# The causal mask of the self attention as a bf16 product on TensorE instead of a minimum on VectorE

## What is computed

```python
def attn(x, qkv_w, o_w):
    b, s, d = x.shape
    hd = d // H
    qkv = (x @ qkv_w.T).reshape(b, s, 3, H, hd).transpose(2, 0, 3, 1, 4)
    q, k, v = (qkv[0], qkv[1], qkv[2])
    a = jnp.einsum('bhqd,bhkd->bhqk', q, k) * hd ** (-0.5)
    mask = jnp.triu(jnp.ones((s, s), dtype=bool), 1)
    a = jax.nn.softmax(jnp.where(mask, -1000000000.0, a), axis=-1)
    out = jnp.einsum('bhqk,bhkd->bhqd', a, v).transpose(0, 2, 1, 3).reshape(b, s, d)
    return out @ o_w.T
...
x = x + attn(rmsnorm(x, n1_w), qkv_w, o_w)
x = x + moe(rmsnorm(x, n2_w), gate_w, up_w, down_w)
```

## Time and profile before

| | |
|---|---|
| median of three runs | 2839.97 us |
| profiled execution | 2830.95 us |
| its span, first to last instruction | 2829.7 us |
| mean granted clock of TensorE | 0.975 |
| TensorE matmuls busy | 2597.7 us, 92% |
| VectorE busy | 2187.3 us, 77% |
| ScalarE busy | 1684.6 us, 60% |
| GpSimd busy | 1134.9 us, 40% |
| minimum with the mask, L727 | 64 instructions, 78.3 us, from 1326.6 to 2562.1 us |

### The profile page before, as it was taken

How to read it: one execution, slowest core, us unless ns; L and a number is a source line. 1 busy time by engine, 2 the same in 40 slices (tenths; PEclk the granted TensorE clock), 3 DMA queues, 4 the chain that set the end, 5 groups by cost and what they waited for, 6 DMA issues and landing times.

```text
span 2829.7 us, 60900 instructions
## 1 busy us (share of the span) xinstructions
PE 2597.7 (92%) x23748; PEld 2122.2 (75%) x23748; DVE 2187.3 (77%) x4794; ACT 1684.6 (60%) x4539; POOL 1134.9 (40%) x1981
## 2 busy tenths in 40 slices
PE   7797989899888989999899999999999999999999
PEld 5676767677666767777777777888787878788777
DVE  7868697877678587786767777787878787778998
ACT  4565666666555666666555555655656565656544
POOL 2132323323443543324454444333333333435676
PEclk9898999999899999999999999999999999999999
DMA  6000000000011121100012121100000000000110
GB/s 189 3 24 9 18 13 18 14 13 18 11 48 40 63 77 42 30 16 24 11 46 62 55 76 58 33 19 20 21 16 21 16 24 13 24 3 25 33 36 21
DMA packets 84168, 92.15 MB, mean 33 GB/s; under 512 B 15332, under 2 KB 77288, under 8 KB 83880
## 3 DMA queue, kind: packets, MB, share of 16 engines
q1 hardware_dynamic: 75432, 59.91, 6.9%
q0 software_dynamic: 8448, 28.34, 3.4%
HBM read 65.36 MB, written 22.85 MB: 31 GB/s over the span
## 4 chain that ended last, share of the span: by engine, by line
PE 63%; DVE 23%; ACT 5%; POOL 4%; issue 3%; DMA 1%; SPq 1%; DVEq 0%; POOLq 0%; ACTq 0%
PE psum L353 14%; PE psum L377 12%; PE psum L346 12%; PE psum L403 6%; DVE tiny L730 4%; PE psum L415 3%; PE psum L532 3%; DVE big L738 3%; PE psum L370 3%; PE psum L360 3%; PE psum L367 2%; PE psum L526 2%; PE psum L513 2%; DVE xn L711 1%; DVE tiny L766 1%
## 5 line engine op out<-in xcount | busy, mean ns | idle before, releaser
L377 PE MATMUL psum<-ident,big 128*128 128x128 f32 x2784 | 428.2, 285 | 66.2 <-ACT big L1219 22.4
L377 PEld LDWEIGHTS psum<-ident,big 128*128 128x128 f32 x2784 | 324.0, 145 | 140.2 <-ACT big L1219 49.3
L1219 ACT ACTIVATE big<-big 128x512 f32<-128x512 f32 x512 | 312.1, 631 | 170.4 <-DVE big L738 168.5
L730 DVE TENSOR_REDUCE tiny<-psum 128x8 f32<-128x1024 f32 x256 | 312.3, 1220 | 47.5 <-PE psum L403 42.8
L738 DVE TENSOR_TENSOR big<-psum,tiny 128x512 f32<-128x512 f32 x512 | 329.6, 685 | 8.8
L1382 POOL TENSOR_SCALAR tiny<-mv 128x1 f32<-128x1 f32 x224 | 53.0, 236 | 677.1 <-DVE mv L701 674.9
L403 PE MATMUL psum<-head_keys,small 64*128 64x256 f32 x2048 | 285.9, 403 | 19.7 <-ACT big L1226 10.9
L1399 POOL TENSOR_TENSOR head_keys<-big,head_rows 128x512 f32<-128x512 f32 x256 | 266.6, 1060 | 0.0
L1424 POOL TENSOR_TENSOR big<-big,tiny 128x512 f32<-128x512 f32 x128 | 133.8, 1052 | 308.2 <-DVE tiny L773 308.0
L403 PEld LDWEIGHTS psum<-head_keys,small 64*128 64x128 f32 x2048 | 185.3, 189 | 74.6 <-issue 56.9
L1263 ACT ACTIVATE big<-psum,tiny 128x128 f32<-128x128 f32 x512 | 181.7, 382 | 38.1 <-DVE tiny L768 37.6
(11 more groups left out here) (334 smaller groups left out, 6616.7 us busy)
## 6 DMA issues: line engine op xcount, KB each, us to landing
ctxT<-in_ctxT SPq DMA_DIRECT2D x64, 128.0 KB, 2.2
after_L_xattn<-x SPq DMA_DIRECT2D x64, 128.0 KB, 1.7
mixture_out<-spare SPq DMA_DIRECT2D x46, 128.0 KB, 1.7
x_in<-in_x SPq DMA_DIRECT2D x32, 128.0 KB, 2.2
mixture_in<-xn SPq DMA_DIRECT2D x32, 128.0 KB, 1.7
x_in<-after_L_xattn SPq DMA_DIRECT2D x32, 128.0 KB, 2.1
w_bits<-after_L_xattn SPq DMA_DIRECT2D x32, 128.0 KB, 2.1
spare<-in_L_w SPq DMA_DIRECT2D x2, 1024.0 KB, 7.2
```

Source lines behind the costliest of these rows:

```text
L377: last = pe.transpose(bank[:, k * P:(k + 1) * P], src[:, k * P:(k + 1) * P], identity)
L730: dve.tensor_reduce(top, s8, AX.X, ALU.max).then_inc(*t.dve.tell(p, f"{l}.top{r}"))
L1219: last = act.activation(flat, flat, ACT.Exp, scale=DH ** -0.5)
```

## The change

The minimum on VectorE is gone, with its signal. In its place TensorE lays the mask first: for each group of eight scores of the self attention it multiplies the bf16 identity by `m.future`, a bf16 tile of four copies of the mask (0 where a key may be seen, -4e9 where not), into each of the two banks, 128 x 512 each, with the start flag. The score products then accumulate on it. `m.future` is made once in the setup by one more VectorE instruction. The turns in `ORDER` stand in another sequence on all five engines, with the same number of turns for each lane; of these only the place is marked here.

```diff
@@ SPREAD @@
-SPREAD = {"L2": "clip", "self": "mask"}
+SPREAD = {"L2": "clip"}
@@ ORDER @@
...
@@ pe_heads @@
             pe.wait_ge(*t.act.at(p, f"{l}.eT1"))
+        if l == "self":
+            for half in range(2):
+                pe.matmul(t.ab[:, half, :], m.ident_bf[:], m.future[:].rearrange("p h s -> p (h s)"), start=True, stop=False)
         keys = t.head_keys[r].rearrange("p h s -> p (h s)")
         for cols in (slice(0, D), slice(D, 2 * D)):
             for half in range(2):
                 rows = slice(half * P // 2, (half + 1) * P // 2)
-                last = pe.matmul(t.ab[:, half, cols], t.qT[rows, r, :], keys[rows, cols], start=True, stop=True)
+                last = pe.matmul(t.ab[:, half, cols], t.qT[rows, r, :], keys[rows, cols],
+                                 start=l != "self", stop=l != "self" or cols.start > 0)
@@ dve_heads @@
-        if l == "self":
-            dve.tensor_tensor(s8, s8, m.causal[:].rearrange("p (o s) -> p o s", o=1).to_broadcast([P, 2 * CH, S]),
-                              ALU.min).then_inc(*t.dve.tell(p, f"{l}.mask{r}"))
-            dve.wait_ge(*t.dve.at(p, f"{l}.mask{r}"))
         dve.tensor_reduce(top, s8, AX.X, ALU.max).then_inc(*t.dve.tell(p, f"{l}.top{r}"))
@@ dve_constants @@
     dve.tensor_scalar(m.before[:], m.causal[:], 0.0, None, ALU.is_le)
+    dve.tensor_scalar(m.future[:], m.causal[:].rearrange("p (o s) -> p o s", o=1).to_broadcast([P, CH, S]), 0.0, None, ALU.min)
@@ shared_memory @@
+    m.future = sb("future", [P, CH, S], BF16)
```

More of the change, by code:

```diff
@@ L172 @@
[L172 to L176, removed]
@@ new lines @@
+        "1310112320023023002312310320212312021013320232120333122030132231011010130333122212001203120032010303"
+        "1221032132321212310300201313133231201201310210313023202011321123020303220230303021202332132102330120"
+        "2122303131300021020331033210010111200120323023010131230232302001023323213121313103022132021102130320"
+        "1131012312023130203011301122030230212003130212320210330123223203103010213332130102011112310302020130"
+        "2101032132323221212312313132332323002001312312312311212013201312123210301131130220332023221201203303"
@@ new lines @@
+        "1232220300301302131121330033210201221102130230210301120212300231031203020103010302101203001301313313"
+        "3221031020213130232010230211213201301212131302312103110323002202023023123212010033022322301303103103"
+        "0101330233021221220010212103023010130212020102200310031232132133011022121031213021203010232112120210"
+        "1213212013301230022011032131230232033313031322022010331311010303030230120310321001013313310021020200"
+        "2313113100220023121322130203201101302031120132231001232013121010202012111012232103110221303123212312"
@@ new lines @@
+        "0313130202221012313223201033032210020233130320123010310202201121323311312131212313232121233322323230"
+        "2000323120311300120231100201031220130312130100202231320212121231033032113023032210020113221231003012"
+        "2012030211130231203012332031321030130312310012131030303010203211213230121000123022133231001303122310"
+        "0213203301210201232120100212101210122120301220110102320231300202131231003011010323101212320210331032"
+        "0320323012232003123203231003202102013310301210133210130303031303211221020123101333002030102210313213"
@@ new lines @@
+        "1202102332032113231320211203213210120103302202301221110020231230023110310332101203232310132031013023"
+        "2032101321232002132032310002330230102133013132103103001023101033313120231321002010223012103313223213"
+        "1023201200113231321312120312211123031022301310212330203211013313001303120302101220230132230302133322"
+        "1002023312323010313021022023113030031321132031201210012032210020133132231300302012012023132313010021"
+        "2101213220121113221323202112030103332112200213310131323003021203012303122320210323020310201202332310"
@@ new lines @@
+        "0310310320110201323331123010103130121032201201303223203021320203120130312323101201013122132033213211"
+        "1323123021132130310303102322020101323100132203102113031202320212303203023122103013012002311333010320"
+        "1120230312132021010330230322123010231201323300201312010202311302203131213102023230123121132313031130"
+        "3032022213003013120010130323102102330321231130232012021030123213310132002330310120330103231231231213"
+        "0310012203278087223002708232007872878039a09730a7098a739a98a90a807893a079a789a303a9783a7098a987033739"
@@ new lines @@
+        "1121032330321323223010230330012130101100230221233233031032013012010310113233102311212203212302202010"
+        "3030301231378783207873802337382a97a98709a987a09a089a907a807398a0777a9a089878370909a09a78a39789a73bac"
+        "b98c70cbac8b98a97cab780bac9b8ca89a7bc978a87a89a09cb9c0b65956b9bc6b9c65cb659bc965bc689a856abc57b68756"
+        "c9b5c65796abc65b5a65ab6b95ab659c7965c7b68bc786cb5ca56c68a5cb69b6c9a6ba59a65b68c8b56c5875c87b58b57b76"
+        "57c6a5ac7658a7c8c567c865b5cb7c575b6c576b6ab56a5cb67ac587968cb95b685a96ca5bc9769858a65c69856"
@@ L268 @@
[L268 to L271 removed]
+        "1203332223111100023112210313223301011221131231122002322333331020300010100112233110331211211100223130"
```

170 lines of the change are left out of this document (72 added, 98 removed).

## The result

The changed kernel takes 2844.01 us (median of 20 runs, 2839.78 to 2851.94) against 2838.38 us for the kernel before on the same chip: ratio 1.0020, 95% interval 1.0013 to 1.0027, 5.6 us slower. So it is slower by 0.2 to 0.4%. The forecast was +15 us.

The account below looks back on a forecast made before the run. TensorE, 95% busy in the self attention's stretch, was taken as the bound. Added work of 31.4 us less 16 given back makes +15.4 us, 2855 us against the median 2839.97; 8 in 10 range 2832 to 2875.

Parts of the forecast that it names:

- the mask's own sum: Self attention's stretch: 31.4 us of TensorE work added, 16 us of idle time given back, net +15.4 us.
- Products 0.22 us each: TensorE, ahead of the self scores: 128 bf16 products of 512 columns at 0.22 us, 28.2 us in all.
- Weight loads at nothing: TensorE: the products' 128 weight loads hide behind the matmul ahead; without that cover at most 14 us.
- The rival of cheap wide products: TensorE: 512 columns cost no more than 256, products 14.1 us instead of 28.2, time 2841; chance 0.05.
- Added TensorE work: TensorE: products 28.2, switches of form 2.7 and setup 0.5 us, 31.4 us on an engine 95% busy.
- Switches of form: TensorE, full-array mask beside half-array scores: up to 19 of 64 groups add 0.29 us each; 2.7 us taken.
- Given back: Self attention's softmax: each lane's path shortens by 0.83 us per group, so TensorE's idle time falls by 16 us.
- The rest: Setup instruction 0.5 us; the new turns on all queues, priced in the first half, plus or minus 6 us, zero in the middle.
- Nothing is given back: TensorE's idle time stays because the order, not VectorE, makes it: 2871 us; chance 0.15.
- The lanes' latency decides: Four lanes each bound by their own path, -13 us each; TensorE 98% busy, time 2827; chance 0.12.
- It comes out even: 24.6 us of mask leave the chain, the new work lands on it only partly: about 2837; chance 0.15.
- Waits for L1219: Expected sign: the transposes' waits for ScalarE's exp in the self attention's stretch fall by some 15 us.

Follow-up runs that it names:

- e1: The changed kernel (mask as TensorE product) with the turns of the kernel before on all five queues: 2855.22 us, ratio 1.0058 to the kernel before.
- e3: The kernel before with no causal mask at all, neither minimum nor product, old turns: ratio 0.9962 to the kernel before.
- e15: e1 with 38 swaps of neighbouring turns on ScalarE only: ratio 1.0069 to the kernel before.
- e2: The kernel before, minimum still on VectorE, with the changed kernel's turns on all five queues: ratio 1.0193 to the kernel before.
- e4: The changed kernel with no causal mask at all, neither minimum nor product, new turns: ratio 0.9995 to the kernel before.
- e10: The changed kernel with 47 swaps of neighbouring turns where an engine idled while the next turn was ready: ratio 0.9997 to the kernel before.
- e13: e10 with 30 more swaps by the same rule, from its own trace: ratio 0.9988 to the kernel before.
- e5: e1 with 77 of the 128 turns of self attention's transposes one place earlier on TensorE: ratio 1.0157 to the kernel before.
- e7: The changed kernel with 125 turns of self attention's transposes one place later on TensorE: ratio 1.0167 to the kernel before.
- e16: e1 with 52 swaps of neighbouring turns on VectorE only: ratio 1.0159 to the kernel before.
- e8: The kernel before with the mask as a GpSimd multiplication after the exp, old turns plus 128 on GpSimd: ratio 1.0274 to the kernel before.

## Why the prediction was right in part and wrong in part

**Right: the mask's own sum.** With the turns held fixed, the sum of +15.4 us meets +15.05 us by the medians (e1) and +16.5 (12.8 to 20.2) by the ratio. Part of that is luck, because the minimum and the product, taken apart by e3, are each worth 4 to 5 us less than their terms, and the two misses cancel. Term by term:
- Products 0.22 us each: 0.216 us apart. Weight loads at nothing: 98 ns each in the median, and they do not widen that distance. The rival of cheap wide products is out.
- Added TensorE work 31.4 us in all: 31.6 us more busy time in the stage, but some 3 us of it are other work that the new turns bring in, so the close match is chance as well. In the pair with the old turns, e3 and e15, it is 31.0 us. Switches of form: of the 64 groups of self scores 14 follow another half-array product in the records of before, 21 of the mask products do after, where I had up to 19 and took half. What was measured of the price is 0.09 us one way, of the 0.29 us estimated for there and back.
- Setup 0.5 us: 0.42.
- Given back 16 us: in e1 less. The product's 31 us and the net of 16.5 leave 15; e3, which takes the minimum away and adds nothing, gains only 10.8 (6.8 to 14.8), and the product's 27.3 us by e1 minus e3 is 4 us under its work. The two readings differ by less than their intervals; 16 fits the first and lies above the second's. By TensorE's idle time it is 10 us (65.2 before, 54.9 in e15).
- First part unchanged, clock at its level, tail unchanged: all seen.

**Wrong: the step "The rest", the new turns at plus or minus 6 us with zero in the middle.** They took back 5 to 11 us, and this is the whole miss of 4 to 10 us. I looked for their effect in the first part, where TensorE idles most and the mask isn't; there they did nothing that can be told. They act in the stage that has the mask. My step "Given back" let the path of each lane shorten by 0.83 us as soon as the minimum goes, as if engines took work when it is ready. They take it by turn: in e1 the path shortens by 0.12 to 0.19 us, because the exp ends 1.93 us after the subtraction instead of 0.76. Under the new turns the path is 6.45 us. That the shorter path is what saves the time isn't shown, for e2 and e4 have shorter paths as well and are slower than their like with the old turns. What is shown is the pairing: the new turns are no part that stands beside the mask, to be priced by itself: alone they cost 55 us (e2), with no mask they cost 9 (e4 against e3), with the product they gain. As a term the order had to stand as part of "given back" and not beside it; the runs put it at 5 to 11 us for the product.

**The rivals.** "Nothing is given back" is out: idle time fell by 21 us. "The lanes' latency decides" is out as a time, -12 us; its mechanism, idle time that takes in the new work, is what the new turns bring in part (15 us of idle time filled, above): TensorE at 97%, not 98%. "It comes out even" gave 2837. By time the result lies between it and the forecast, and by e10 and e13 it is reached with 47 to 77 more swaps; but its reason, that the chain loses 24.6 us, isn't what happened, for with the turns held the minimum was worth 10.8 us.

**Expected signs.** TensorE over 96% busy: 97%. VectorE's 78 us: by 79.0 with the old turns (e1, 2187.3 to 2108.3 us), by 61 with the new ones. Waits for L1219 down by 15 us: 32.0 + 12.7 fell to 16.2 + 7.2, 21 us.

**What isn't settled.** How the new turns save their 5 to 11 us, and how much of it falls to which engine: TensorE or VectorE moved by hand alone (e5, e7, e16) only lose, ScalarE alone (e15) changes nothing that can be told. And why the swap rule helps one sequence and hurts another.

## What to carry to other kernels

Where each engine's sequence is fixed, an operation that changes engine is only half an edit: run the new code with the old sequence and the old code with the new one as well, for the sum of the parts doesn't hold (here +16 and +55 make +6 to +11). Time taken from a step in the middle of a lane's path was swallowed here by the unchanged turns of the next two engines (8.40 to 8.28 us), and hand-made shifts on one engine cost from nothing to 42 us. A shorter path of one layer is no forecast of the time either: judge a sequence by the kernel's time. Price a matmul by the distance between starts (0.216 us here, 0.38 us in the records), don't take TensorE's busy time for its work, and check the stage's length in two profiles before reading a few microseconds off it.

## What the runs showed that was not expected

- Records of matmuls go missing in a pattern. By tile, e1 has all 128 weight loads of the products and 68 of the matmuls:

```profile
L401 PEld LDWEIGHTS psum<-future,ident_bf x128: 95/98/181, 1322.8 to 2582.9; 128*128 128x128 bf16 x128
L401 PE MATMUL psum<-future,ident_bf x68: 377/379/390, 1323.2 to 2583.1; 128*128 128x512 bf16 x68
```

  Its stage has x11774 matmuls beside x11833 loads, so TensorE's busy time in it, 1303.1 of 1364.4 us, is too short. The modelled end of the matmul ahead covers most of a missing product: the gap that is left is 53 ns in most of the 60 places and 6 us in all at most. So the idle time is 55 us or more where the view says 61. The counts of loads and matmuls, side by side, show when this is so; in the stages of before and after they agree within 3.
- The same VectorE instructions take longer under the new turns. The costliest of them are 256 of L817, in the first half; before (old turns), then e2 (new turns, same code), with the duration min/median/max by line below each:

```profile
L817 DVE SCALAR_TENSOR_TENSOR big<-big,w_conv 128x127 f32<-128x127 f32 x256 | 76.5, 361 | 10.3 <-ACT big L1288 10.2
L817 DVE SCALAR_TENSOR_TENSOR big<-big,w_conv x256: 317/344/1129, 69.9 to 1252.9; 128x127 f32<-128x127 f32 x128
```
```profile
L817 DVE SCALAR_TENSOR_TENSOR big<-big,w_conv 128x127 f32<-128x127 f32 x256 | 85.4, 395 | 14.6 <-ACT big L1288 14.4
L817 DVE SCALAR_TENSOR_TENSOR big<-big,w_conv x256: 318/345/1691, 71.6 to 1261.7; 128x127 f32<-128x127 f32 x128
```

  The median stays and the mean rises, so a few get much longer; in after the maximum is 1655 ns, and its VectorE as a whole is 18 us busier than e1's. It cost nothing that can be told, for the first part is as long as before. The traces tell what goes with it. 9 of the 256 take over 450 ns before, 21 after and in e2, and every one of them overlaps a tensor_tensor of GpSimd of over 600 ns; those that overlap none stay between 317 and 365 ns. Such a place in after, four L817 in 2.91 us instead of 1.4:

```profile
1002.75 2.04 POOL L1400 TENSOR_TENSOR head_keys<-big,head_rows 128x512 f32<-128x512 f32 x2
1003.34 2.91 DVE L817 SCALAR_TENSOR_TENSOR big<-big,w_conv 128x127 f32<-128x127 f32 x4 [1.12 <-ACT big L1289]
```

  e8 is the test of it, though it was made for something else: against e3 it has 128 more such instructions on GpSimd and the same work on VectorE, and VectorE's busy time rises from 2108.3 to 2126.7 us. More than half of that falls to the norm (e3, then e8), in which the 13 that overlap the new multiplication take 1.24 us on average and the others 0.56:

```profile
L711 DVE TENSOR_SCALAR xn<-x,mv,tiny 128x256 f32<-128x256 f32 x192 | 106.5, 555 | 62.4 <-POOL tiny L1381 61.9
```
```profile
L715 DVE TENSOR_SCALAR xn<-x,mv,tiny 128x256 f32<-128x256 f32 x192 | 116.5, 607 | 71.9 <-POOL tiny L1385 71.5
```

  The subtraction L738, which reads PSUM, takes 686 ns in both. So the new turns lay more of VectorE's work beside GpSimd's.
- 52 swaps of neighbouring turns among VectorE's 2291 cost 1% of the kernel (e16 against e1, 29 us), more than all the idle time that the change took from TensorE.
- GpSimd's multiplication in place of 128 x 512 fp32 took 1.27 us on average, the spreading of the keys of the same size 1.07 us in the changed kernel; I had counted 1.05.
